# Second layer of a two-layer vision tower: two halves of the tokens in one interleaved order of all engines, the image mask as three contraction rows, values scaled on ScalarE

## What is computed

```python
# second attention, 12 heads of 16, within each image, ternary weights
xn = rmsnorm(layernorm(h2)); s = 127 / max|xn|; xq = round(xn * s)          # integers, one scale a token
q, k, v = (xq @ ternary(w_qkv)) / s
o = softmax(q @ k.T / 4) @ v                                                 # keys of the same image only
h3 = h2 + (round(rmsnorm(o) * s2) @ ternary(w_proj)) / s2
# second feed-forward part: 8 experts of width 128 and a shared one
x4 = layernorm(h3); scores = sigmoid(x4 @ gate)                              # two experts out of the two best groups
out = h3 + shared(x4) + sum_e weight_e * ((silu(x4 @ w1[e]) * (x4 @ w3[e])) @ w2[e])
```

## Time and profile before

| what | value |
|---|---|
| runs: median (lowest to highest of 3) | 459.07 us (458.83 to 459.37) |
| profiled execution, its own time | 458.68 us |
| span in the profile, first to last instruction | 456.8 us, 7260 instructions |
| busy, share of the span: PE, PEld, DVE, ACT, POOL | 87%, 61%, 51%, 27%, 21% |
| mean granted clock of PE | 0.944 |
| padding matmuls (line 470) in the whole program | 256, 64.3 us |

### The profile page before, as it was taken

The page is one execution under the profiler, slowest core; times in us unless marked ns, Lnnn a source line. Parts: engine busy times, 40 slices in busy tenths (PEclk is TensorE's granted clock), DMA queues, the critical chain, the costliest instruction groups (busy, mean ns, idle before and its releaser), DMA issues.

```text
span 456.8 us, 7260 instructions
## 1 busy us (share of the span) xinstructions
PE 395.3 (87%) x2795; PEld 276.9 (61%) x2795; DVE 233.6 (51%) x649; ACT 123.0 (27%) x349; POOL 93.8 (21%) x105
## 2 busy tenths in 40 slices
PE   0479997999998999997998999697899976979996
PEld 0477456565455557844987999243577743556664
DVE  3727506859354443471435222258677697074444
ACT  0234420021237782102322332002433411311110
POOL 1401300226314432004357452100000011000000
PEclk9999999999999999998999999798759796889999
DMA  8940000035000000194598721550000000000001
GB/s 243 347 113 2 0 1 1 1 102 209 2 1 1 1 1 1 30 330 148 169 300 248 271 62 39 147 197 1 0 1 1 1 1 1 0 1 1 0 2 40
DMA packets 16463, 34.52 MB, mean 76 GB/s; under 512 B 3355, under 2 KB 8907, under 8 KB 16299
## 3 DMA queue, kind: packets, MB, share of 16 engines
q1 hardware_dynamic: 14545, 29.64, 20.2%
q0 software_dynamic: 1824, 4.36, 3.2%
q10 hardware_dynamic: 58, 0.03, 0.0%
HBM read 31.01 MB, written 3.13 MB: 75 GB/s over the span
## 4 chain that ended last, share of the span: by engine, by line
PE 66%; DVE 18%; ACT 5%; issue 4%; DMA 4%; POOL 1%; SPq 1%; DVEq 0%; POOLq 0%
PE slot L470 6%; PE slot L682 5%; PE slot L380 5%; PE slot L364 4%; PE slot L696 4%; PE slot L614 4%; PE slot L688 3%; PE slot L408 3%; ACT area_e L1123 3%; PE slot L630 3%; PE slot L569 3%; PE slot L384 3%; PE slot L548 2%; PE slot L765 2%; PE slot L506 2%
## 5 line engine op out<-in xcount | busy, mean ns | idle before, releaser
L470 PE MATMUL slot<-ident_bf 128*128 128x512 bf16 x256 | 64.3, 404 | 8.3 <-issue 3.9
L949 POOL TENSOR_TENSOR rstd<-var_eps,half_neg 111x3 f32<-111x3 f32 x20 | 17.3, 866 | 198.6 <-DVE var_eps L1292 96.2
L470 PEld LDWEIGHTS slot<-ident_bf 128*128 128x128 bf16 x256 | 25.0, 102 | 39.2 <-issue 11.4
L1613 DVE TENSOR_TENSOR area_c<-area_c,slot 128x384 f32<-128x384 f32 x19 | 10.5, 554 | 51.6 <-ACT area_c L1186 41.0
L1036 POOL DMA_INDIRECT ys_dram<-area_c,area_d x19 | 21.7, 1143 | 33.4 <-DVE area_c L1622 33.4
L1123 ACT ACTIVATE area_e<-slot,nmax 111x111 f32<-111x111 f32 x72 | 24.2, 376 | 9.6 <-DVE nmax L1433 9.6
L1433 DVE TENSOR_REDUCE nmax<-slot 111x6 f32<-111x666 f32 (+2 forms) x24 | 19.8, 845 | 12.2 <-PE slot L765 7.4
L1641 DVE TENSOR_TENSOR area_c<-area_c,slot 128x333 f32<-128x333 f32 (+1 forms) x18 | 7.5, 460 | 31.6 <-ACT area_c L1201 31.6
L1021 POOL DMA_INDIRECT area_c<-xs_dram,area_d x19 | 18.6, 980 | 21.2 <-DVE area_d L1547 15.7
L614 PE MATMUL slot<-x_t,area_a 128*128 128x333 f32 (+1 forms) x64 | 19.6, 451 | 2.9 <-DVE area_c L1641 2.9
L548 PE MATMUL slot<-consts_sb,area_e 111*111 111x111 f32 x144 | 20.7, 305 | 0.8 <-POOL area_e L1006 0.8
(11 more groups left out here) (259 smaller groups left out, 774.4 us busy)
## 6 DMA issues: line engine op xcount, KB each, us to landing
area_e<-w_gate_up SPq DMA_DIRECT2D x10, 576.0 KB, 5.1
area_a<-w_gate_up SPq DMA_DIRECT2D x9, 576.0 KB, 4.2
area_w<-w_down SPq DMA_DIRECT2D x13, 288.0 KB, 5.3
area_a<-patches SPq DMA_DIRECT2D x6, 336.0 KB, 5.1
area_e<-w_down SPq DMA_DIRECT2D x6, 288.0 KB, 8.1
area_a<-w SPq DMA_DIRECT2D x1, 1728.0 KB, 9.6
area_c<-ys_dram SPq DMA_DIRECT2D x4, 252.0 KB, 4.4
w_tern_sb<-w_tern SPq DMA_DIRECT2D x1, 864.0 KB, 12.2
```

The source lines that it names most:

```text
L470: mm(bank, ident_bf[:], ident_bf[:].unsqueeze(1).to_broadcast([128, 4, 128]), start=True, stop=True)
```

## The change

1. The second layer no longer takes each step for both halves. PE, ACT and DVE get new lists in which the first half's later steps (projection, last layernorm, routing) stand between steps of the second half's attention, and the feed-forward part goes by 18 units, first the 9 experts for the first half, then the 9 for the second (`UNITS` is 9). What is left of the second half's attention stands in the units 1, 3 and 5 on PE (and near them on ACT and DVE), its routing in unit 10. The routing weights are worked out for each half by itself (`begin_weights`, `end_weights`). POOL's last four powers change order accordingly, and SP waits for the end of each half's units.
2. The mask matmuls of line 760 go, with their constant. Three more contraction rows ride in the projection to queries and keys: a key column gets, for each image of the tile, a large negative number in a spare row of its head unless it belongs to that image, and a query gets a 1 in the row of its own image. The rows come from a new input that SP loads, and ACT makes the two small copies of it in the first layer, before the router's exponential.
3. ACT scales the values (`values3`) and copies all 12 turned blocks of probabilities (`all_turned_probs`); both were DVE's in whole or in part.
4. The padding counts change: 75 to 78 at the start; 8, 18, 12, 5 and 6 later become 17, 4, 8, 4, 3 and 3 at other places.
5. Buffers move: the Silu and product buffers hold a half and lie in `area_w`, the turned integers in `area_b`.

The diff, cut to what the prediction speaks of:

```diff
-              + [(n, g) for n in (RMS_PROJ, LN_H3) for g in range(GROUPS)])
+              + [(n, g) for g in range(GROUPS) for n in (RMS_PROJ, LN_H3)])
...
-        q_int_t = area_d[0:KH, 4 * COLS:6 * COLS].bitcast(BF16).rearrange("p (c n) -> p c n", c=2)
+        q_int_all = area_b[0:KH + PER_TILE, Q_AT:Q_AT + 2 * COLS].bitcast(BF16).rearrange("p (c n) -> p c n", c=2)
...
+            order = [EXPERTS1] + list(range(EXPERTS1))
+            def feed_up(k):
+                g, n = divmod(k, UNITS)
+                slot = take(pe, ("ff", k), ("ff_hidden", k + 1))
+                cols = live_cols(g)
+                packed_pairs([([slot[:, part, 0:cols] for part in range(2)], w13_sb[:, order[n]])],
+                             x_t[:, :, gcols(g, cols)]).then_inc(S["ff_up"], 1)
+            def feed_down(k):
+                g, n = divmod(k, UNITS)
+                slot = take(pe, ("down", k), ("ff_added", k + 1))
+                pe.wait_ge(S["ff_hidden"], k + 1)
+                for i, t in enumerate(group_tiles(g)):
+                    rows = min(ROWS, TOKENS - t * ROWS)
+                    last = mm(by_tile(slot, rows=rows)[:, i, :], hid[:, k % 2, i * ROWS:i * ROWS + rows],
+                              w2_sb[:, order[n], :], start=True, stop=True)
+                last.then_inc(S["ff_down"], 1)
...
+                pe.wait_ge(S["images_marked"], 1)
                 pe.wait_ge(S["ints_t_ready"], g + 1)
+                if g:
+                    keep_warm(8, slot_of[("dq", g)][:, 1, :])
                 for m in range(3):
...
+                        at = b * 384 + m * 128
+                        mm(slot[:, b, 0:COLS], tern_all[:, 0, at:at + 128], q_int_all[:, 0, gcols(g)], start=True, stop=False)
+                        last = mm(slot[:, b, 0:COLS], tern[:, 1, at:at + 128], q_int_t[:, 1, gcols(g)], start=False, stop=True)
                     last.then_inc(S["qk3_done"], 1)
                 project_ints_rows(tern[:, :, 768:960], g, ("v3", g), "v3_done", ("v3_scaled", g + 1))
...
-            def masked_scores3(t):
+            def scores3(t):
...
                 for jp in range(2):
                     slot = take(pe, ("score3", t, jp), ("below_max", 2 * t + jp + 1))
-                    for b in range(2):
-                        mm(slot[0:ROWS, b, 0:COLS], ident_bf[0:ROWS, 0:ROWS], on_tiles(block_bf[:], 3),
-                           start=True, stop=False, skip_group_check=True)
                     for m in range(3):
                         for b in range(2):
                             r = 32 * (2 * jp + b)
                             last = mm(slot[0:ROWS, b, m * ROWS:(m + 1) * ROWS], qk3[r:r + 32, 0, m, tile_cols(t)],
-                                      qk3[r:r + 32, 1, m, tile_cols(t)], start=False, stop=True, skip_group_check=True)
+                                      qk3[r:r + 32, 1, m, tile_cols(t)], start=(m == 0), stop=True, skip_group_check=True)
                     last.then_inc(S["score_done"], 1)
...
-            keep_warm(75)
-            project_ints(0)
-            keep_warm(8)
-            for t in range(TILES):
...
-                if t >= 2:
-                    attend3(t - 2)
-                if t >= 3:
-                    turn_back3(t - 3)
...
-            turn_back3(TILES - 2)
-            turn_back3(TILES - 1)
-            keep_warm(18)
-            turn_ints(0, 2)
-            project_out3(0)
-            keep_warm(12)
-            turn_ints(1, 3)
-            project_out3(1)
-            keep_warm(5)
-            pe.wait_ge(S["w_ff1_loaded"], 64)
-            order = [EXPERTS1] + list(range(EXPERTS1))
-            def w13(n):
-                return w13_sb[:, order[n]]
-            shared = []
-            for g in range(GROUPS):
-                if g:
-                    keep_warm(6)
...
+            keep_warm(78)
+            project_ints(0)
+            pe.wait_ge(S["q3_copied"], 1)
+            keep_warm(17, slot_of[("qk3", 0, 0)][:, 0, :])
+            scored(0)
+            scores3(0)
+            keep_warm(4)
+            project_ints(1)
+            scores3(1)
+            turn_probs(TILES, 0)
+            scores3(2)
+            turn_probs(TILES, 1)
+            scored(1)
+            scores3(3)
+            turn_probs(TILES, 2)
+            scores3(4)
+            attend3(0)
+            attend3(1)
+            attend3(2)
+            turn_back3(0)
+            turn_back3(1)
+            turn_back3(2)
+            turn_probs(TILES, 3)
+            keep_warm(4, slot_of[("probs_t", TILES + 3, 1)][:, 1, :])
+            attend3(3)
+            turn_probs(TILES, 4)
+            scores3(5)
+            keep_warm(3)
+            turn_ints(0, 2)
+            keep_warm(3, slot_of[("probs_t", TILES + 4, 1)][:, 1, :])
+            project_out3(0)
+            attend3(4)
+            turn_probs(TILES, 5)
+            turn_back3(3)
+            turn_back3(4)
+            attend3(5)
+            turn_ff_rows(0)
+            turn_back3(5)
+            router_logits1(0)
+            feed_up(0)
+            beside = {1: lambda: turn_ints(1, 3), 3: lambda: project_out3(1), 5: lambda: turn_ff_rows(1),
+                      10: lambda: router_logits1(1)}
+            for k in range(1, GROUPS * UNITS + 1):
+                if k < GROUPS * UNITS:
+                    feed_up(k)
+                if k in beside:
+                    beside[k]()
+                feed_down(k - 1)
...
+            load(wt_all[KH:, :, 0:768], tern_masks, "tern_masks_loaded")
...
-                sp.wait_ge(S["ff_added"], GROUPS * (EXPERTS1 + 1) - (GROUPS - 1 - g))
+                sp.wait_ge(S["ff_added"], (g + 1) * UNITS)
...
-            nc.gpsimd.tensor_copy(block_bf[:], const("block", ROWS))
...
-            for norm in (RMS_PROJ, LN_H3):
-                for g in range(GROUPS):
+            for g in range(GROUPS):
+                for norm in (RMS_PROJ, LN_H3):
                     power(norm, g)
...
+            act.wait_ge(S["tern_masks_loaded"], 16)
+            fn(tern_all[KH:, 0, 0:768], wt_all[KH:, 0, 0:768], ACT.Copy)
+            images = wt_all[KH:, 1, 0:ROWS]
+            fn(q_int_all[KH:, 0, :].rearrange("p (t n) -> p t n", t=TILES), on_tiles(images, TILES),
+               ACT.Copy).then_inc(S["images_marked"], 1)
...
+            def values3(g):
+                act.wait_ge(S["v3_done"], g + 1)
+                src = by_tile(slot_of[("v3", g)])
+                for i, t in enumerate(group_tiles(g)):
+                    last = fn(v3[:, t, :, 0:HD1], src[:, i, :].rearrange("p (k d) -> p k d", k=HEADS), ACT.Copy,
+                              scale=amax[:, t, 3:4])
+                last.then_inc(S["v3_scaled"], 1)
...
+            def all_turned_probs(t):
+                n = TILES + t
+                act.wait_ge(S["probs_turned"], 2 * n + 1)
+                act.wait_ge(S["attended"], n - PB + 1)
+                fn(pt_buf[:, n % PB, 0:8, :].rearrange("p (b i) x -> p b (i x)", b=2),
+                   slot_of[("probs_t", n, 0)][0:ROWS, :, 0:4 * ROWS], ACT.Copy).then_inc(S["probs_t_kept0"], 1)
+                turned_probs(n)
...
+            scales_and_queries(0)
+            values3(0)
+            scales_and_queries(1)
+            exps3(0)
+            values3(1)
+            exps3(1)
+            all_turned_probs(0)
+            exps3(2)
+            all_turned_probs(1)
+            all_turned_probs(2)
+            exps3(3)
+            columns3(0)
+            columns3(1)
+            exps3(4)
+            columns3(2)
+            all_turned_probs(3)
+            columns3(3)
+            all_turned_probs(4)
+            int_columns(2, 0)
+            exps3(5)
+            columns3(4)
+            all_turned_probs(5)
+            columns3(5)
+            columns(("x4_t", 0), "x_turned", 7, 0, x_t, "x_t_ready")
+            sigmoids1(0)
+            beside = {1: lambda: int_columns(3, 1),
+                      5: lambda: columns(("x4_t", 1), "x_turned", 8, 1, x_t, "x_t_ready"), 10: lambda: sigmoids1(1)}
+            for k in range(GROUPS * UNITS):
+                silu(k)
+                if k in beside:
+                    beside[k]()
+            act.wait_ge(S["ff_added"], GROUPS * UNITS)
...
+                for i, t in enumerate(group_tiles(g)):
+                    rows = min(ROWS, TOKENS - t * ROWS)
+                    weight = comb1[0:rows, t, n - 1:n] if n else 1.0
+                    last = v.scalar_tensor_tensor(h[3][0:rows, t, :], by_tile(slot_of[("down", k)], rows=rows)[:, i, :],
+                                                  weight, h[3][0:rows, t, :], ALU.mult, ALU.add)
+                last.then_inc(S["ff_added"], 1)
...
-            keys_and_values3(0)
+            keys3(0)
             quantised_rows(1)
             below_max3(0)
-            keys_and_values3(1)
-            for t in range(TILES):
-                if t >= 1:
-                    below_max3(t)
-                if t >= 1:
-                    turned_probs(TILES + t - 1)
-                if t >= 3:
```

(49 more changed lines are left out.)

237 lines of the change are left out of this document (71 added, 166 removed).

## The result

The changed kernel takes **433.55 us** (median of 432.63 to 440.19), the kernel before took 459.22 us beside it: a ratio of 0.9435, 95% interval 0.9406 to 0.9463. The prediction was 433.5 us. The profiled execution took 434.38 us for a span of 432.6 us, against 458.68 and 456.8 us. On the chip of most experiments the executions of the kernel before scattered from 446.34 to 464.43 us, with mean clocks from 0.971 to 0.923, and with the undisturbed executions of both kernels the ratio there is 0.9697 (0.9646 to 0.9748).

What follows compares the result with a forecast made beforehand. No one engine bounds the layer: both halves step together, each step waiting for its slowest engine. 458.68 - 28.9 - 1.6 = 428.2, plus 4.9 for the clock and 0.4 to the median: 433.5 us; range 427.0 to 441.5.

Steps and rivals of the forecast that it cites:

- Start, first scores, tile 1: Second layer's opening: 78 paddings set the start at 310.05 us; first scores at 318.2, scores of tile 1 at 327.2.
- clock term: Scores 1 to 4 and tiles 0 to 2: 17 us at the lower level add 4.8 us to 18.2, giving 23.0.
- rival A: Clock stays up in the attention, with no PE wait over 1.3 us left: 428.6 us; chance 0.22.
- ScalarE ends a wait among the scores: Sign named beforehand, in the new profile's second-layer scores, by which the prediction would be wrong; no size given.
- B: Rival: clock stays low through the attention, costing 10.3 us, 438.9 us in all; chance 0.28.
- To the first expert: After the first tiles, a DVE chain, then PE turns, ScalarE copies, PE routes: 19 us, attention of tiles 3 to 5 beside it.
- The experts: 18 half units cost 50.8 us like 9 experts; second-half steps 4.6, waits 3.7, last addition 1.2: 60.3 us.
- in all 3.7 us: PE's waits for DVE in the experts: second half's integers 0.8, routing 0.5, 0.8 and 1.4, normalised rows 0.3.
- the 1.6 us: Correction taken off the whole sum: the same durations carried through the old order ended 2.0 us late over 144 us.
- I take nothing: Image mask as three more contraction rows on a 96-row matmul: no added time, 0.06 us a half if time followed rows.
- D: Rival: an overlooked wait in the in-order queues or the ring of four slots joins the halves again: 459 us; chance 0.01.
- C: Rival: PE waits for Silu and product in each half unit, the experts' clock falls, 36 us more: 469 us; chance 0.04.

Runs made afterwards that it cites:

- experiment 2: Changed kernel with 52 paddings ahead of the second layer in place of 78: 428.12 us against 434.63.
- the repeat: The changed kernel unaltered, run again on the chip of most experiments: 434.63 us (432.67 to 438.25).
- experiment 1: Changed kernel with eight paddings in PE's 1.98 us wait for the second layer's first exponentials: 432.32 us; with further paddings ahead of later turns and weighted values: 435.62 us.
- Experiment 6: Changed kernel taking two half units' up-projections together, then two down-projections: 441.88 us; with routing and second-half steps spread over more pairs: 445.78 us.
- experiment 4: Changed kernel with 24 mask matmuls and 96 contraction rows again: 435.22 us; kernel before with only the three mask rows added: 449.91 us beside 456.98.
- experiment 3: Changed kernel with the second half's turn, projection, normalised rows and router ahead of the first expert, its VectorE routing left in units 10 and 11: 448.78 us.

## Why the prediction was right

**Start, first scores, tile 1: right.** Predicted 310.05, 318.2 and 327.2 us; measured 310.27, 317.98 and 326.80. That the start fits is partly luck: the paddings began 1.44 us later than before, and 78 of them took 18.70 us where the sum has 19.92. "Nothing else is on the chip there" was wrong: DVE makes its whole numbers and two diagonals until 303.55 us in the kernel before and then waits 6.46 us for PE, which experiment 2 takes back. ScalarE's scaling took 1.05 us (taken 1.0), the wide copy 0.91 (taken 1.1), and a matmul with 99 contraction rows 0.30 to 0.31 us, as with 96.

**Scores and first tiles: near, with a clock term that was partly luck.** With 4.8 us for the clock the stretch was to take 23.0 us; it took 348.75 - 326.80 = 21.95, with exactly the 17 us at the lower level that were carried over from the same stage before. That the number came again is luck: the repeat had 13.7 us in the whole attention stage. Without the lower level it takes 18.0 us (346.43 - 328.44 in experiment 1; predicted 18.2), so the term is 3.95 us. But rival A's ground, "no PE wait over 1.3 us is left", was wrong: 1.98 us are left, because ScalarE's 1.28 us table load for the exponentials stands between its last copies of queries and the first exponentials. The load was counted in the experts and not looked for here, though the trace of the kernel before has it at the same place, at 329.12 us. By the prediction's own words, that ScalarE ends a wait among the scores was to mean that it is wrong, and on this path it was. Rival A's price, 428.6 us, is what executions at a higher clock came to (427.89 us in experiment 1, with the wait filled); B did not come: the clock rose at 347 us. By the rule of the Trainium skill that B was weighed with ("TensorE: Matmul & The Clock Gate", section "Part 4: PE-mode transpose": transposes do not count as busy for the clock as other matmuls do) one would look for a low stretch from 329 to 347 us of experiment 1 as well, since it holds three turns and no padding behind the first eight; that trace has 1.00 there, with turns at 1.42 us, and does not agree. Scores and weighted values stand between these turns, so turns by themselves were not tried. In the changed kernel only 2 x 0.43 x 4 = 3.4 us more were low, from 360 to 364 us.

**To the first expert: right in size.** 19 us were predicted; 368.58 - 348.75 = 19.83 with those 3.4 us in it. The path is not DVE's chain to its end: DVE has the normalised rows at 363.23 us, but PE comes to turn them only at 364.17, behind tile 5's turn and the work after it, which were to lie beside the chain.

**The experts: right in the sum, wrong in two terms that cancel.** Predicted 60.3 us, measured 60.94. "50.8 us ... the same matmuls" is the step that failed: the single units of the changed kernel take more. Of the chain of waits:

```profile
395.98 1.12 PE slot L385 x4
397.10 0.76 PE slot L389 x4
397.86 1.16 PE slot L628 x6
...
409.20 1.07 PE slot L385 x4
410.28 0.64 PE slot L389 x4
410.91 1.28 PE slot L628 x6
412.19 1.07 PE slot L385 x4
```

A unit of each half is 3.04 and 2.99 us, together 6.03 against 5.64 in the earlier trace rows: the half-row stages take 1.40 against 1.20 us, the down-projections 2.44 against 2.25, the full-row ones 2.19 in both. Nine times 0.39 is 3.5 us. Experiment 6 shows that the half-row part goes when two units share a stage (from 432.10 to 433.18 us, 1.08 us for two of the second half, against 2 x 0.64), and that the second half's down-projections stay at 2 x 1.28 us when paired (from 433.18 to 435.74 us). On the other side "in all 3.7 us" of PE's waits was too much: PE waited 0.42 us for the second half's integers and 0.38 for its projection, and for the routing not at all, since its two parts (373.53 to 376.25 and 376.71 to 379.33 us on DVE) lie behind products that PE already had.

**The sum: the close hit is luck.** No run shows the 1.6 us that were taken off because the same durations, carried through the old order, ended late. Without them the sum puts the last addition at 424.7 + 4.9 = 429.6 us, and it ended at 429.52. The traced execution then took 434.38 us and not 433.1; the median comes out at 433.55 because it lies 0.83 us under the traced execution, where 0.4 us above it was taken.

**The mask: "I take nothing" holds for the rows.** That the removed mask matmuls could matter for the clock stood only as a ground against A; the traces of experiment 4 fit it and do not show it by itself.

**D and C fell.** Undoing the overlap costs 14 to 15 us (experiment 3), about 4 of them by the clock, so it is the larger part of the 13 to 14 us that the change is worth at like clocks. C's mechanism, waits in the units that bring the clock down, is not in the changed kernel but was met in experiment 6, at 10 us and not 36.

## What to carry to other kernels

When a chain of small steps on one engine keeps another on paddings, split the tokens and put one half's chain under the other half's matmuls; price it by the waits and by the clock that falls in them. Before a gain is put down to an edit, compare executions at like clocks: here that leaves 13 to 14 us of 24 to 26. Look again at paddings that stand at the head of a chain of waits: 26 fewer were worth 5.6 us here, and nothing else was touched. And before packing matmuls more tightly, look at who fills the gap when the other engine is late: 0.4 us saved in a pair cost 10 us in waits and clock.

## What the hardware showed that was not expected

- The same kernel has its low stretches in different places in different executions: the attention stage of the unaltered changed kernel had 20.9 us at the lower level in one trace and 13.7 in the other, and with its longest wait filled there were none in two traces and about 10 in a third.
- In the attention stage a microsecond at the lower level costs 0.21 to 0.24 us, not half a microsecond, as PE has waits to give; in experts with PE full, eight matmuls took 4.13 us in place of 2.40.
- Adding 24 mask matmuls left the median within 1 us, with the stage's clock in the one trace at 0.98 in place of 0.75 and 0.83.
- A down-projection whose last tile has 37 rows takes 1.28 us of the chain of waits against 1.16 us for three full tiles, and the full-row matmuls behind it 1.07 us against 0.87 behind a full one (259 columns both); together that is 2.35 against 2.03 us.
